# First attention layer of an eight-layer kernel: who masks the early times, and with what

## The chip, the cores and the metric

The kernel runs on one core of one Trainium2 chip. The metric is the time of one execution in microseconds (us) on the device; lower is better. The core's engines each run their own instruction stream: TensorE (PE in the profile), VectorE (DVE), ScalarE (ACT), GpSimd (POOL), and SyncE (SP), which here issues the DMAs. They meet at semaphores: an instruction adds to one when it has finished, and a `wait_ge` holds one engine's stream until the semaphore has reached a value. Everything behind a wait on the same engine waits too.

## The reference

Eight layers follow one another on a residual stream of 2048 times by 128 channels. Only the first, a windowed attention, is touched. Cut to what matters, it computes:

```
delta, nh, bd, hs = 64, 16, 16, 8
disp = (x @ W_disp)  ;  val = (x @ W_val)            # per head
strain = disp[t - delta + 1 + d] - disp[t]           # for d in 0..63
bond_logits = gelu(strain @ W_strain + rel_emb @ W_pos) @ W_bond
damage = sigmoid(gelu(strain @ W_dmg + b_dmg) @ W_dmg_out + b_dmg_out)
logits = bond_logits - 10 * damage
cmask = t - delta + 1 + d >= 0
logits = where(cmask, logits, -inf)
out = softmax(logits, over d) @ windows of val
```

The mask matters only where t is below 63, that is in the first block of 128 times: there, positions d that would lie before time 0 must not count.

## The kernel before, in words

The layer is `bond_attention`. After a set-up (constants, weights, a layer norm and a transpose) one large block does all the work. It is cut into 8 phases, numbered p = 0 to 7: four chunks of 512 times, and for each two halves of the heads (8 heads each, `HH`). A phase has 32 steps (`TPP`), numbered 0 to 31 here, in four groups of 8 (`TPG`). A step makes one tile of differences, 128 partitions by 4 x 512 elements. The whole run of 256 steps is one order that every engine follows.

In each group, steps 0 to 3 are made by GpSimd (L601, one instruction each, into `l0a_diff_pool`) and steps 4 to 7 (`D_AT`) by VectorE (L580, four instructions each, into `l0a_diff_dve`). Each of the two has a ring of four buffers, and may refill one only when TensorE has reduced what was in it. ScalarE takes the tiles strictly in the order of the steps and applies Gelu in place (L633); TensorE reduces each (L455, eight matmuls). After step 5 of the next group VectorE writes a group's logits to `l0a_logits` (L495).

The softmax of a phase is done while the next phase runs. In the loops of TensorE and VectorE a function `tail` says at which step of the phase each part of it is put in. TensorE transposes the logits of the phase before, one block of 128 times after each of steps 5 to 8 (L384). VectorE's `subtract_max` runs at steps 13 to 16, one block b = 0 to 3 each: a maximum over d (L508), then the difference (L510) from PSUM into the SBUF tile `l0a_exps` (E in the code). It is emitted ahead of VectorE's own difference tile of the same step. ScalarE takes the exponential of all four blocks ahead of step 18 (L609), with a table load on either side. SyncE then writes E to a band in DRAM and reads it back, and TensorE transposes what came back (L392) at steps 28 to 31 and 0 to 3, with VectorE's copies (L518) at steps 4 to 11. ScalarE also makes, ahead of step 26, the tile `l0a_a_of_t` (L616) without which GpSimd can't begin step 0 of the phase after.

The mask: the block b = 0 of the two phases of the first chunk (p = 0 and 1, so in the loop while phases 1 and 2 run) holds the early times. There `subtract_max` first copies the transposed logits from PSUM to E (L505), and GpSimd, which has no access to PSUM in this code, masks E in place with an `affine_select` (L592). GpSimd's stream has this at step 5 of phases 1 and 2, that is between its tile of step 3 and its tile of step 8, with a wait on the copy. VectorE makes that copy at its own step 13. After the mask VectorE takes the maximum and the difference from E in SBUF.

Of the kernel before, what the change touches and what calls it, by code (L numbers as in the profile page):

```python
# [5 lines left out]
P = 128  # L6
# [9 lines left out]
ALU = mybir.AluOpType  # L16
ACT = mybir.ActivationFunctionType
AX = mybir.AxisListType.X
NEG = -1.0e30
# [150 lines left out]
def bond_attention(nc, g, I):  # L170


    NH, HS, BD, W = 16, 8, 16, 64
    HH = P // BD
# [5 lines left out]
    TPP = GPP * TPG  # L180
# [5 lines left out]
    with ExitStack() as ctx:  # L186
        r = Room(nc, ctx, "l0a")
# [10 lines left out]
        V = r.sb("val", [P, TB, NH, HS + 1])  # L198
        VS = r.sb("val_shifted", [P, TB, NH, HS + 1])
        zero = r.sb("zero", [P, HH * UB])  # L200
        band = nc.dram_tensor("l0a_band", [2, 4, P, UB * HH], F32, kind="Internal").ap()
        band_zeroed = r.sem("band_zeroed")
        with ExitStack() as ctx2:
# [35 lines left out]
            sel, zr = r2.sem("mask_steps"), r2.sem("zeroed")  # L239
            with nc.Block() as block:  # L240

                @block.vector
                def _(dve):
                    dve.memset(zero[:, :], 0.0).then_inc(zr, 1)
                    dve.memset(wbs[:, :, :, :], 0.0)
                    dve.memset(A[:, :, :, 0:PAD], 0.0)
                    dve.memset(V[:, :, :, HS:HS + 1], 1.0)
                    dve.memset(VS[:, :, :, HS:HS + 1], 1.0)
                    dve.memset(VS[0:W, 0, :, 0:HS], 0.0)

                @block.gpsimd
                def _(pool):
                    pool.memset(bm[:, :], 1.0).then_inc(sel, 1)
                    pool.wait_ge(sel, 1)
                    pool.affine_select(out=bm[:, :], in_=bm[:, :], compare_op=ALU.is_ge, fill=0.0, base=0,
                                       pattern=[[-BD, HH]], channel_multiplier=1).then_inc(sel, 1)
                    pool.wait_ge(sel, 2)
                    pool.affine_select(out=bm[:, :], in_=bm[:, :], compare_op=ALU.is_ge, fill=0.0, base=BD - 1,
                                       pattern=[[BD, HH]], channel_multiplier=-1)

                @block.sync
                def _(sp):
                    sp.wait_ge(zr, 1)
                    for par in range(2):
                        for b in range(4):
                            sp.dma_start(band[par, b], zero[:, :]).then_inc(band_zeroed, 16)
# [45 lines left out]
        E = r.sb("exps", [P, 4, W, HH])  # L312
# [9 lines left out]
        at_ready, atb_ready = r.sem("a_of_t_in_psum"), r.sem("a_of_t_in_sbuf")  # L322
        filled, emptied = r.sem("ring_filled"), r.sem("ring_emptied")
        maxd, expd = r.sem("max_done"), r.sem("exp_done")
        raw, masked = r.sem("first_block_copied"), r.sem("first_block_masked")
        written, loaded = r.sem("band_written"), [r.sem("band_loaded%d" % b) for b in range(4)]
        v_ps, inv, o_done = r.sem("values_in_psum"), r.sem("sums_inverted"), r.sem("o_done")
        ot_ps, ot_sb, y_ps, x_done = r.sem("oT_in_psum"), r.sem("oT_copied"), r.sem("y_in_psum"), r.sem("x_added")
# [4 lines left out]
        def use(*key):  # L333
            return uses.setdefault(key, len(uses))

        def bank(n):
            return g.ps[:, n * CH:(n + 1) * CH]

        def slot(s):
            i = s // TPG * len(D_AT) + D_AT.index(s % TPG) if s % TPG in D_AT else s // TPG * NP_ + s % TPG  # L340
            return (dd[:, i % ND, :, :], diff_dve, i) if s % TPG in D_AT else (dp[:, i % NP_, :, :], diff_pool, i)

        def place(s):
            p, rest = divmod(s, TPP)
            dg, rest = divmod(rest, TPG)
            k, n = divmod(rest, 4)
            return p, p // 2, p % 2, dg, k, n

        def window(s):
            p, q, hf, dg, k, n = place(s)  # L350
            first = A[:, hf, k, q * CH + 16 * dg + n + 1:q * CH + 16 * dg + n + 2]
            return bass.AP(first.tensor, first.offset, [list(first.ap[0]), [4, 4], [1, CH]])

        with nc.Block() as block:

            @block.tensor
            def _(pe):
# [90 lines left out]
                for s in range(NT):  # L448
                    p, q, hf, dg, k, n = place(s)
                    ge, _, _ = slot(s)  # L450
                    pe.wait_ge(gelu_done, s + 1)
                    if n == 0 and s >= TPG:
                        pe.wait_ge(tanh_done if k == 0 else logit_done, s // TPG)
                    for c in range(4):
                        mm = pe.matmul(g.ps[32 * c:32 * c + 32, (2 + k) * CH:(3 + k) * CH], wbs[:, k, n, :], ge[:, c, :],  # L455
                                       start=(n == 0), stop=(n == 3))
                    mm.then_inc(reduced, 1)
                    tail(p, s % TPP)
# [5 lines left out]
            def _(dve):  # L464
# [33 lines left out]
                def subtract_max(p, b):  # L498
                    u = use("l", p, b)
                    dve.wait_ge(filled, u + 1)  # L500
                    if b == 0 and p >= 1:
                        dve.wait_ge(written, 32 * p)
                    raw_l = bank(RING[u % len(RING)]).rearrange("p (d h) -> p d h", h=HH)
                    if p // 2 == 0 and b == 0:
                        dve.tensor_copy(E[:, 0, :, :], raw_l).then_inc(raw, 1)  # L505
                        dve.wait_ge(masked, p + 1)
                        raw_l = E[:, 0, :, :]
                    dve.tensor_reduce(mx[:, b, :], raw_l.rearrange("p d h -> p h d"), AX, ALU.max).then_inc(maxd, 1)  # L508
                    dve.wait_ge(maxd, LB * p + b + 1)
                    dve.tensor_tensor(E[:, b, :, :], raw_l, mx[:, b, :].unsqueeze(1).broadcast_to([P, W, HH]),  # L510
                                      ALU.subtract).then_inc(emptied, 1)
# [53 lines left out]
                for s in range(NT):  # L565
                    p, q, hf, dg, k, n = place(s)
                    if s % TPP == 0:
                        a_of_t(p)
                    tail(p, s % TPP)
                    if s % TPG not in D_AT:  # L570
                        continue
                    out, _, i = slot(s)
                    if s % TPP == D_AT[0]:
                        dve.wait_ge(at_ready, p + 1)
                    if i >= ND:
                        dve.wait_ge(reduced, (i - ND) // ND * TPG + D_AT[i % ND] + 1)
                    src = window(s)
                    for c in range(4):
                        d = 16 * dg + 4 * c + n
                        ins = dve.scalar_tensor_tensor(out[:, c, :], src[:, c, :], pos[:, d:d + 1], bank(1), ALU.add, ALU.subtract)  # L580
                    ins.then_inc(diff_dve, 1)
# [4 lines left out]
            @block.gpsimd  # L586
            def _(pool):
                for s in range(NT):
                    p, q, hf, dg, k, n = place(s)
                    if s % TPP == 5 and 1 <= p <= 2:  # L590
                        pool.wait_ge(raw, p)
                        pool.affine_select(out=E[:, 0, :, :], in_=E[:, 0, :, :], compare_op=ALU.is_ge, fill=NEG,  # L592
                                           base=1 - W, pattern=[[1, W], [0, HH]], channel_multiplier=1).then_inc(masked, 1)
                    if s % TPG in D_AT:
                        continue
                    out, _, i = slot(s)
                    if s % TPP == 0:
                        pool.wait_ge(atb_ready, p + 1)
                    if i >= NP_:
                        pool.wait_ge(reduced, (i - NP_) // NP_ * TPG + i % NP_ + 1)  # L600
                    pool.tensor_tensor(out, window(s), atb[:, p % 2, :].unsqueeze(1).broadcast_to([P, 4, CH]),  # L601
                                       ALU.subtract).then_inc(diff_pool, 1)
# [1821 lines left out]


LAYERS = (bond_attention, masked_ffn, mamba, gated_experts, dual_attention, ternary_ffn, plain_attention, int8_ffn)


# [58 lines left out]
```

## Time and profile before

| | us |
|---|---|
| median of 3 runs | 3114.46 |
| lowest and highest | 3110.84, 3115.29 |
| the profiled execution | 3105.74 |
| its span in the trace | 3103.7 |
| block of the first attention in the trace (8 phases, then the last softmax) | 39.8 to about 645 |
| busy over the whole span: PE, DVE, ACT, POOL | 77%, 62%, 64%, 34% |

The busy shares are means over eight layers with different limits, so they do not say what the first one is worth; for that the block has to be read by itself. In the block POOL is busy for 534 us. An engine that ends an instruction frees the next one's start, and for pipelined instructions the end of one and the start of the next can overlap by some 0.1 us.

### The profile page before, as it was taken

Reading aid. Unit: us, or ns where it says so; the run is one execution under the profiler, and the core shown is the slowest. Engines: PE = TensorE matmul, PEld = TensorE weight load, DVE = VectorE, ACT = ScalarE, POOL = GpSimd, SP = SyncE. Lnnn points to the kernel's source line nnn. Section 1 sums busy time; section 2 is a strip of 40 time slices with the busy share of each in tenths; the row PEclk is TensorE's granted clock in tenths of the full one; section 3 lists DMA queues with packets and bytes.
Section 4 is the critical chain, followed back from the end, with each engine's and each line's share of the span. In section 5 each row is a group of like instructions: output and inputs, shape, how many; then the busy total and the mean of one; then the engine's idle time right before and its main releaser. Section 6 shows DMA issues by size and latency. Waiting matters only on the chain. (4 is left out here: it accounts for less than half of the span.)

```text
span 3103.7 us, 32934 instructions
## 1 busy us (share of the span) xinstructions
PE 2384.6 (77%) x12512; PEld 823.1 (27%) x12512; DVE 1938.8 (62%) x2732; ACT 1977.1 (64%) x1894; POOL 1068.9 (34%) x404
## 2 busy tenths in 40 slices
PE   3577777756546676755799988999769859999995
PEld 1122222333112222322222242222434412222223
DVE  5777988758699999887598907986350430121115
ACT  4789999912523333212499947997522249999991
POOL 5889999711079998621000400013000000000000
PEclk8889999979678888887899999999889879999998
DMA  2011121110044544201301020001010030111000
GB/s 72 1 41 41 44 77 43 41 51 8 7 159 156 172 156 153 71 9 54 63 11 26 11 39 1 11 13 43 7 39 0 20 75 14 31 29 26 14 6 27
DMA packets 67032, 144.68 MB, mean 47 GB/s; under 512 B 15607, under 2 KB 30032, under 8 KB 66161
## 3 DMA queue, kind: packets, MB, share of 16 engines
q1 hardware_dynamic: 66864, 142.46, 16.4%
q8 instruction: 103, 1.69, 0.2%
q14 instruction: 65, 0.52, 0.1%
HBM read 117.99 MB, written 24.25 MB: 46 GB/s over the span
## 5 line engine op out<-in xcount | busy, mean ns | idle before, releaser
L601 POOL TENSOR_TENSOR l0a_diff_pool<-l0a_A,l0a_a_of_t 128x2048 f32<-128x2048 f32 x128 | 532.4, 4197 | 34.8 <-ACT l0a_a_of_t L616 34.8
L1604 ACT ACTIVATE l2x_pT<-ps 128x1024 f32<-128x1024 f32 x512 | 495.8, 1021 | 7.3 <-PE ps L1563 5.4
L1604 ACT ACTIVATE l3he_pT<-ps 128x1024 f32<-128x1024 f32 x512 | 496.0, 1021 | 4.1 <-PE ps L1563 2.2
L1069 PE MATMUL ps<-l1s_hc,all_ident 128*128 128x512 f32 x512 | 283.7, 707 | 182.6 <-POOL l1s_hc L1040 100.3
L580 DVE SCALAR_TENSOR_TENSOR l0a_diff_dve<-l0a_A,l0a_pos,ps 128x512 f32<-128x512 f32 x512 | 344.7, 740 | 44.2 <-PE ps L455 44.1
L1031 POOL TENSOR_TENSOR l1s_dBx<-l1a_dtx,l1s_Bs 128x1024 f32<-128x1024 f32 x128 | 297.4, 2353 | 133.3 <-DMA l1s_Bs<-l1a_bc 133.3
L1055 ACT ACTIVATE ps<-l1a_dt,l1a_A 128x1024 f32<-128x1024 f32 x128 | 143.1, 1118 | 274.0 <-DVE l1s_hc L1100 219.9
L1667 DVE COPY l3he_oT<-ps 128x512 f32<-128x512 f32 x16 | 11.1, 691 | 445.2 <-PE ps L1577 445.1
L1563 PE MATMUL ps<-l3h_Qs,l3h_Ks 75*128 75x512 bf16 x1024 | 267.8, 385 | 24.5 <-DVE ps L1652 24.5
L1563 PE MATMUL ps<-l2m_Qs,l2m_Ks 75*128 75x512 bf16 x1024 | 270.2, 388 | 9.8 <-PEq L1886 9.8
L633 ACT ACTIVATE l0a_diff_pool<-l0a_diff_pool 128x2048 f32<-128x2048 f32 x128 | 237.7, 1901 | 53.9 <-POOL l0a_diff_pool L601 53.8
L1577 PE MATMUL ps<-l2x_pT,l2m_Va 128*9 128x512 f32 x2048 | 269.0, 598 | 1.2 <-ACT l2x_pT L1604 1.2
L1577 PE MATMUL ps<-l3he_pT,l3h_Va 128*9 128x512 f32 x2048 | 268.4, 596 | 0.6 <-ACT l3he_pT L1604 0.6
L455 PE MATMUL ps<-l0a_diff_pool,l0a_reducers 128*32 128x512 f32 x1024 | 158.2, 702 | 119.3 <-ACT l0a_diff_pool L633 118.1
L2028 POOL TENSOR_TENSOR l2s_E<-l2s_E,l2x_rest 128x2048 f32<-128x2048 f32 x16 | 72.7, 4545 | 510.6 <-DVEq L1752 505.5
L633 ACT ACTIVATE l0a_diff_dve<-l0a_diff_dve 128x2048 f32<-128x2048 f32 x128 | 237.2, 1897 | 0.3
L1713 DVE TENSOR_SCALAR_CACHE_REDUCE l2x_rest<-l2s_E,l2x_at 128x2048 f32<-128x2048 f32 x96 | 225.2, 2346 | 3.4
L1069 PEld LDWEIGHTS ps<-l1s_hc,all_ident 128*128 128x128 f32 x512 | 109.1, 224 | 357.9 <-POOL l1s_hc L1040 133.4
L455 PE MATMUL ps<-l0a_diff_dve,l0a_reducers 128*32 128x512 f32 x1024 | 150.0, 664 | 50.3 <-ACT l0a_diff_dve L633 48.8
L1563 PEld LDWEIGHTS ps<-l3h_Qs,l3h_Ks 75*128 75x128 bf16 x1024 | 79.8, 98 | 305.3 <-ACT l3he_pT L1604 218.9
L1563 PEld LDWEIGHTS ps<-l2m_Qs,l2m_Ks 75*128 75x128 bf16 x1024 | 80.4, 98 | 292.6 <-ACT l2x_pT L1604 218.3
L1100 DVE TENSOR_TENSOR l1s_hc<-ps,l1s_Cs 128x1024 f32<-128x1024 f32 x86 | 105.3, 1224 | 1.8 <-issue 0.3
(404 smaller groups left out, 3321.8 us busy)
## 6 DMA issues: line engine op xcount, KB each, us to landing
l1s_Bs<-l1a_bc SPq DMA_DIRECT2D x64, 512.0 KB, 3.7
l1s_Cs<-l1a_bc SPq DMA_DIRECT2D x64, 512.0 KB, 4.7
l0a_band_rows<-l0a_band SPq DMA_DIRECT2D x32, 512.0 KB, 5.3
l0a_band<-l0a_exps SPq DMA_DIRECT2D x16, 512.0 KB, 5.1
l2m_Ks<-l2m_parts SPq DMA_DIRECT2D x36, 128.0 KB
l2m_Qs<-l2m_parts SPq DMA_DIRECT2D x72, 64.0 KB
l3h_Ks<-l3h_parts SPq DMA_DIRECT2D x36, 128.0 KB
l3h_Qs<-l3h_parts SPq DMA_DIRECT2D x72, 64.0 KB
```

Of the source, the lines that this page charges most:

```text
L455: mm = pe.matmul(g.ps[32 * c:32 * c + 32, (2 + k) * CH:(3 + k) * CH], wbs[:, k, n, :], ge[:, c, :], start=(n == 0), stop=(n == 3))
L580: ins = dve.scalar_tensor_tensor(out[:, c, :], src[:, c, :], pos[:, d:d + 1], bank(1), ALU.add, ALU.subtract)
L601: pool.tensor_tensor(out, window(s), atb[:, p % 2, :].unsqueeze(1).broadcast_to([P, 4, CH]), ALU.subtract).then_inc(diff_pool, 1)
L633: act.activation(ge, ge, ACT.Gelu).then_inc(gelu_done, 1)
L1031: pool.tensor_tensor(db[:, m % NDB, :], dtx[:, i, h, half * TH:(half + 1) * TH], Bs[:, k % NBS, :], ALU.mult).then_inc(dbd, 1)
L1055: act.activation(hpair(m), dt[:, i, h, half * TH:(half + 1) * TH], ACT.Exp, scale=Al[:, i, h, n:n + 1]).then_inc(dad, 1)
L1069: mm = pe.matmul(g.ps[:, (4 + 2 * h + q) * CH:(5 + 2 * h + q) * CH], g.ident[:, :], hc[:, m % NHC, q * CH:(q + 1) * CH], start=(n == 0), s ...
L1100: dve.tensor_tensor(hc[:, m % NHC, :], hpair(m), Cs[:, k % NCS, :], ALU.mult).then_inc(weighed, 1)
L1563: mm = pe.matmul(g.ps[:, slot * QC + c * CH:slot * QC + (c + 1) * CH], hd.Ks[:, hg % 2, j, kt * P:(kt + 1) * P], hd.Qs[:, qc, j, c * CH:(c ...
L1577: mm = pe.matmul(g.ps[32 * j:32 * j + HS + 1, ACC + c * CH:ACC + (c + 1) * CH], hd.Va[:, kt, hg * 4 + j, :], pT[:, (4 * n + j) % NPT, c * ...
L1604: act.activation(pT[:, turn % NPT, :], g.ps[:, slot * QC:(slot + 1) * QC], ACT.Exp).then_inc(expd, 1)
L1713: step(dve.tensor_scalar(junk[:, b % 2, :], E[:, b, :], at[:, 0, b:b + 1], 0.0, ALU.is_ge, ALU.add, accum_out=at[:, 1, b:b + 1]))
```

## The change

The tile `early_mask` (128 x 64: 0 where the position counts, -1e30 where it does not) is made once in the layer's set-up block by GpSimd, with a memset and an `affine_select`. In the loop VectorE no longer copies the logits to E; it adds the mask tile, repeated over the heads, to them on the way from PSUM to E. GpSimd's `affine_select` and its wait on the copy are gone from its stream, and the semaphore for that copy with them. The maximum and the difference from E stay.

```
+        early = r.sb("early_mask", [P, W])
...
+                    pool.memset(early[:, :], 0.0).then_inc(sel, 1)
+                    pool.wait_ge(sel, 3)
+                    pool.affine_select(out=early[:, :], in_=early[:, :], compare_op=ALU.is_ge, fill=NEG, base=1 - W,
+                                       pattern=[[1, W]], channel_multiplier=1)
...
                     if p // 2 == 0 and b == 0:
-                        dve.tensor_copy(E[:, 0, :, :], raw_l).then_inc(raw, 1)
+                        dve.tensor_tensor(E[:, 0, :, :], raw_l, early[:, :].unsqueeze(2).broadcast_to([P, W, HH]),
+                                          ALU.add).then_inc(masked, 1)
                         dve.wait_ge(masked, p + 1)
                         raw_l = E[:, 0, :, :]
...
-                    if s % TPP == 5 and 1 <= p <= 2:
-                        pool.wait_ge(raw, p)
-                        pool.affine_select(out=E[:, 0, :, :], in_=E[:, 0, :, :], compare_op=ALU.is_ge, fill=NEG,
-                                           base=1 - W, pattern=[[1, W], [0, HH]], channel_multiplier=1).then_inc(masked, 1)
```

## Rows read from the trace of the kernel before

**Rows 1.** Waits in 30 to 645 us: who waited for whom, total, times, longest.

```profile
POOL l0a_exps L592 <- DVE l0a_exps L505: 25.9, 2, 13.5
```

**Rows 2.** Timeline of POOL: start, us, instruction, count, [idle before it, and who ended it].

```profile
39.80 82.90 POOL L601 TENSOR_TENSOR l0a_diff_pool<-l0a_A,l0a_a_of_t 128x2048 f32<-128x2048 f32 x20 [31.47 <-ACT l0a_a_of_t L616]
135.12 1.09 POOL L592 TENSOR_SCALAR_AFFINE_SELECT l0a_exps<-l0a_exps 128x512 f32<-128x512 f32 x1 [12.42 <-DVE l0a_exps L505]
136.17 50.16 POOL L601 TENSOR_TENSOR l0a_diff_pool<-l0a_A,l0a_a_of_t 128x2048 f32<-128x2048 f32 x12
186.78 16.67 POOL L601 TENSOR_TENSOR l0a_diff_pool<-l0a_A,l0a_a_of_t 128x2048 f32<-128x2048 f32 x4 [0.45 <-ACT l0a_a_of_t L616]
...
217.96 50.16 POOL L601 TENSOR_TENSOR l0a_diff_pool<-l0a_A,l0a_a_of_t 128x2048 f32<-128x2048 f32 x12
268.57 66.52 POOL L601 TENSOR_TENSOR l0a_diff_pool<-l0a_A,l0a_a_of_t 128x2048 f32<-128x2048 f32 x16 [0.46 <-ACT l0a_a_of_t L616]
335.67 66.49 POOL L601 TENSOR_TENSOR l0a_diff_pool<-l0a_A,l0a_a_of_t 128x2048 f32<-128x2048 f32 x16 [0.58 <-ACT l0a_a_of_t L616]
```

**Rows 3.** Windows over phases 1, 2, 3: length, busy by engine, PE clock, DMA share, GB/s.

```profile
106.90:186.80 79.90, 49.13 (x272) 8.99 (x272) 54.37 (x78) 63.30 (x40) 67.03 (x18) 0.75 0.13 40
186.80:268.60 81.80, 54.63 (x452) 18.16 (x448) 61.94 (x91) 65.68 (x41) 67.89 (x18) 0.83 0.12 39
268.60:335.70 67.10, 50.33 (x456) 18.29 (x452) 59.87 (x94) 65.45 (x41) 66.52 (x17) 1.00 0.15 48
```

**Rows 4.** Timeline of ACT in phase 4, steps 11 on, to the next phase.

```profile
436.11 1.91 ACT L633 ACTIVATE l0a_diff_pool<-l0a_diff_pool 128x2048 f32<-128x2048 f32 x1 [1.53 <-POOL l0a_diff_pool L601]
437.93 3.69 ACT L633 ACTIVATE l0a_diff_dve<-l0a_diff_dve 128x2048 f32<-128x2048 f32 x2
...
442.10 3.87 ACT L633 ACTIVATE l0a_diff_dve<-l0a_diff_dve 128x2048 f32<-128x2048 f32 x2
445.87 3.70 ACT L633 ACTIVATE l0a_diff_pool<-l0a_diff_pool 128x2048 f32<-128x2048 f32 x2
...
469.10 0.71 ACT L616 ACTIVATE l0a_a_of_t<-l0a_A,l0a_minus_bd 128x512 f32<-128x512 f32 x1
```

**Rows 5.** Timeline of DVE in phase 4, steps 13 to 15.

```profile
431.47 0.69 DVE L495 SCALAR_TENSOR_TENSOR l0a_logits<-l0a_tanh,ps 128x512 f32<-128x512 f32 x1 [0.72 <-PE ps L455]
432.07 0.68 DVE L508 TENSOR_REDUCE l0a_maxima<-ps 128x8 f32<-128x512 f32 x1
...
433.40 2.72 DVE L580 SCALAR_TENSOR_TENSOR l0a_diff_dve<-l0a_A,l0a_pos,ps 128x512 f32<-128x512 f32 x4
...
441.31 2.71 DVE L580 SCALAR_TENSOR_TENSOR l0a_diff_dve<-l0a_A,l0a_pos,ps 128x512 f32<-128x512 f32 x4
```

**Rows 6.** Timeline of DVE in phase 1, around the first mask.

```profile
133.68 0.69 DVE L495 SCALAR_TENSOR_TENSOR l0a_logits<-l0a_tanh,ps 128x512 f32<-128x512 f32 x1 [2.46 <-PE ps L455]
134.28 0.68 DVE L505 COPY l0a_exps<-ps 128x512 f32<-128x512 f32 x1
136.24 1.09 DVE L508 TENSOR_REDUCE l0a_maxima<-l0a_exps 128x8 f32<-128x512 f32 x1 [1.27 <-POOL l0a_exps L592]
137.36 3.86 DVE L510 TENSOR_TENSOR l0a_exps<-l0a_exps,l0a_maxima 128x512 f32<-128x512 f32 x1
```

**Rows 7.** Line 510 by form: count, duration ns min/median/max, first and last start.

```profile
L510 DVE TENSOR_TENSOR l0a_exps<-ps,l0a_maxima x30: 690/691/692, 144.5 to 627.3; 128x512 f32<-128x512 f32 x30
L510 DVE TENSOR_TENSOR l0a_exps<-l0a_exps,l0a_maxima x2: 3861/3862/3862, 137.4 to 219.2; 128x512 f32<-128x512 f32 x2
```

**Rows 8.** Timeline of ACT in phase 1: the first Gelu after the mask.

```profile
140.71 1.91 ACT L633 ACTIVATE l0a_diff_pool<-l0a_diff_pool 128x2048 f32<-128x2048 f32 x1 [8.29 <-POOL l0a_diff_pool L601]
```

**Rows 9.** Timeline of PE: one step's eight matmuls, behind its Gelu.

```profile
267.94 1.06 PE L455 MATMUL ps<-l0a_diff_pool,l0a_reducers 128*32 128x512 f32 x8 [0.74 <-ACT l0a_diff_pool L633]
```

**Rows 10.** Timeline of the set-up block: the last mask step of before, and SyncE's DMA issues.

```profile
8.14 0.19 POOL L258 TENSOR_SCALAR_AFFINE_SELECT l0w_bm<-l0w_bm 128x8 f32<-128x8 f32 x1
...
8.93 7.65 SPq L266 DMA_DIRECT2D l0a_band<-l0a_zero  x8
```

More of the change, by code:

```diff
@@ L324, in bond_attention @@
         maxd, expd = r.sem("max_done"), r.sem("exp_done")
-        raw, masked = r.sem("first_block_copied"), r.sem("first_block_masked")
+        masked = r.sem("first_block_masked")
         written, loaded = r.sem("band_written"), [r.sem("band_loaded%d" % b) for b in range(4)]
```

## The prediction

> **What bounds the kernel now.** I read the table of waits over the first attention first. One entry belongs to the changed lines: GpSimd's mask L592 waits for VectorE's copy L505, 25.9 us in two waits [rows 1]. An idle engine costs only if it is the one that paces, so next comes GpSimd's own timeline [rows 2]. It shows an engine with nothing else missing: 20 tiles in one piece from 39.80 to 122.70, then a hole, the mask, 12 tiles, then four tiles to 203.45, a second hole, the mask, 12 tiles, and from phase 3 on 16 tiles in one piece per phase, 66.5 us, with half a microsecond between phases. Phase 3 is 335.67 - 268.57 = 67.10 us long. Phase 1 starts at 122.70 less four tiles (16.6) = 106.1 and lasts to 186.78, so 80.7; phase 2 lasts 81.8. The windows say the same: the same POOL work, 67.0, 67.9 and 66.5 us, in 79.9, 81.8 and 67.1 [rows 3]. So GpSimd stands still in phases 1 and 2, and nothing covers it.
>
> But GpSimd is not alone. The half microsecond at each phase's start is ended by ScalarE's L616 [rows 2], and ScalarE is busy for 65.45 of 67.10 us [rows 3]. The timeline of ScalarE in phase 4, which has the same parity as phase 2, shows how the two share the pace [rows 4]: ScalarE waits 1.53 us for GpSimd's tile of step 11 at 436.11, which is 33.3 us after the phase's start, and from there it runs without a hole to L616 at 469.10, 0.78 before GpSimd can start phase 5. So between step 11 and step 26 ScalarE has no slack: whatever makes it late there moves the next phase by as much.
>
> **The change part by part.** *What goes.* The wait and the mask on GpSimd: from 122.70 to 136.17 is 13.5 us, from 203.45 to 217.96 is 14.5 us [rows 2], 28.0 together (my sum of phase lengths, 80.7 + 81.8 less twice 67.1, says 28.3, the same within reading). This would be the gain if all else went as in phase 3.
>
> *What does not go.* At the masked block VectorE still takes its maximum and difference from SBUF. The maximum takes 1.09 us against 0.68 from PSUM [rows 6, 5]. The difference takes 3.86 us both times, where the 30 that read PSUM take 0.69 [rows 7]. The 3.86 is not work. It was issued at 137.36 and ended at 141.22 [rows 6], while GpSimd's tile begun at 136.17 [rows 2] was just done: ScalarE took it at 140.71 [rows 8]. The difference ended 0.5 us behind that tile, about its own length. So I read it as held until the running GpSimd tile is over. Before, this lay in GpSimd's own hole and cost little; now it stands in the stretch where ScalarE has no slack.
>
> The Trainium skill, page "SBUF — State Buffer", section "SBUF: two separate sides", has a rule for this: VectorE and GpSimd share one pair of SBUF ports as an exclusive lock, which a VectorE instruction with two SBUF inputs needs too, and whoever starts first keeps it for the whole instruction. The trace agrees: 3.86 against 0.69 us. By that rule the difference is held again and the gain is the smaller one below; were there no such lock it would be the full 28.
>
> *Phase 1, worked out.* Until 122.70 nothing changes. GpSimd then makes its tiles of steps 8 to 11 without a hole, the last over by 106.1 + 33.3 = 139.4, so begun at about 139.4 - 4.2 = 135.2. VectorE writes the logits at 133.68 as before, since those depend on ScalarE's steps up to 7. The add starts where the copy did, 134.28. I take 0.69 for it, from the difference that also reads PSUM and an SBUF tile with a repeated dimension [rows 7]; bounds are the copy's 0.68 and the 3.86 of the held one. The maximum starts at 134.95 and ends at 136.05; the wait on `masked` is now one of VectorE for itself, met when the add ends. The difference is issued at 136.1, inside the tile of step 11, and ends at 139.4 + 0.5 = 139.9. Queued behind wait and difference on VectorE are its tiles of steps 13, 14, 15, each with one `subtract_max` in front; steps 13 to 15 start 7.91 us apart [rows 5] and a tile takes 2.71. So they start at 139.85, 143.8 and 147.75, and that of step 15 is ready at 150.45. ScalarE, paced as in phase 4, starts step 11 at 139.4, step 14 at 145.4, step 16 at 139.4 + 9.76 = 149.2 [rows 4]. It needs step 15 at about 147.3; it gets it at 150.5 and reaches step 16 one Gelu (1.8) later, at 152.3: 3.1 late. From there to L616 it is 469.10 - 445.87 = 23.23 us, so 175.5, and GpSimd starts phase 2 at 176.3, where it was 186.78. **Gain 10.5.**
>
> *Phase 2.* In the times of phase 4: logits at 431.47, add at 432.07, maximum at 432.75, difference issued at 433.9, inside the tile of step 11 that is over at 436.05; it ends at 436.6. Tile 13 then starts at 436.55 in place of 433.40, tile 15 at 444.5, ready at 447.2. ScalarE reaches step 16 at 449.05, not 445.87: 3.2 late. The phase is 67.1 + 3.2 = 70.3 in place of 81.8. **Gain 11.5.** Phase 3 starts at 246.6 in place of 268.57.
>
> *The rest at nothing.* GpSimd's ring does not stop it before: for step 24 (155.9 in phase 1) it needs step 16 reduced, at about 155.3 (152.3, a Gelu of 1.9, matmuls of 1.1 [rows 8, 9]), and it ends the phase waiting for L616 anyway. The band's DMAs hang on the exponential, and so do the transposes behind; both move with ScalarE. The two new set-up instructions go behind L258, which ends at 8.33; at 0.2 us each they are done near 8.9, and the block lasts until SyncE has issued its eight DMAs at 16.58 [rows 10]. Without that cover they would cost 0.5. All buffers made after the mask tile move by 256 bytes; no row prices that, and I take nothing.
>
> *Sum.* 10.5 + 11.5 = **22.0 us** less. Against the profiled execution, 3105.74 - 22.0 = 3083.7. That execution is 8.7 below the median of the runs; against the median the forecast is 3114.46 - 22.0 = **3092.5**. Bounds: if the difference is held by nobody and VectorE has slack, nothing is late, gain 28, 3086.4. If the add is held as well, or GpSimd's next tile gets in ahead, each lateness grows by a tile of 4.15, gain 22.0 - 8.3 = 13.7, 3100.8. I take 22.0 since the row that it rests on is the same instruction in the same place, 3.86 both times.
>
> **The rivals.** *The full gain.* VectorE's lateness is absorbed or the difference slips between two tiles: 28.0 less, 3086.4. For it: in phase 1 the issue at 136.1 is only 0.9 behind the change of tiles. Against: in phase 4 even an undelayed tile of step 15 makes ScalarE's pair take 3.87 in place of 3.69 [rows 4], so there is no reserve.
>
> *The clock (slower than before).* TensorE's granted clock was 0.75 and 0.83 in phases 1 and 2 and 1.00 in phase 3 [rows 3]. If the new rhythm left it at the lower level (1.2 GHz) for a phase, phase 3's 50.3 us of matmuls would take up to 100.7, and TensorE would set a phase at 33.6 above 67.1. One such phase in full gives 3114.46 - 22.0 + 33.6 = 3126; it decides from two thirds of a phase on. Against: the low means fall together with the lulls that go away, and the phases without a lull have the high clock.
>
> *Given back.* The gain is there in the block but a stall of the same kind comes behind it, for example GpSimd held at its ring by TensorE late at the masked phases, or a later layer falls on the other clock level: about no change, 3114. Nothing in the rows of phases 3 and 4 shows such a stall, and the layers behind begin from a common barrier.
>
> **How the numbers follow.** My forecast 70 in 100 (its own range 3087 to 3098), full gain 20, given back 6, the clock 4. A difference below 0.2%, 6.2 us, can't be told from none here; so faster 0.90, same 0.06, slower 0.04. The range takes in both bounds, 3086.4 and 3100.8, with some us for the level of the runs, which among themselves spread over 4.5: 3083 to 3102.
>
> **What would show it.** After the change GpSimd should have 20 + 12 tiles in one piece from 39.80 to about 172.6, then a wait of 3 to 4 us for L616; phase 2 should start at 176 and phase 3 at 247. The difference L510 from SBUF should still take 3 to 4 us twice, and ScalarE should wait for VectorE's tiles at steps 14 and 15 by about 3 us in each of the two phases. A phase 2 that starts at 173 says that the lateness is hidden; L510 at 0.69 that nothing holds it; a start past 180 that the add or the ring costs more. The forecast is wrong in kind if phases 3 to 7 are no longer 67.1, or if the time behind the block changes.

## The result and the profile after

The kernel became slower, by 0.4%. Median of 20 runs 3127.99 us (3119.68 to 3145.51), against 3118.95 us (3108.06 to 3127.09) in 20 runs of the kernel before; ratio 1.0036, 95% interval 1.0022 to 1.0049. The forecast was 3092.5, which is 22.0 under the 3114.46 of the three runs known then. The profiled execution took 3119.74 us, its span 3117.6.

The timeline of POOL after the change, which answers to [rows 2]:

```profile
39.86 115.96 POOL L603 TENSOR_TENSOR l0a_diff_pool<-l0a_A,l0a_a_of_t 128x2048 f32<-128x2048 f32 x28 [31.01 <-ACT l0a_a_of_t L618]
176.96 83.53 POOL L603 TENSOR_TENSOR l0a_diff_pool<-l0a_A,l0a_a_of_t 128x2048 f32<-128x2048 f32 x20 [21.14 <-PE ps L460]
263.80 49.91 POOL L603 TENSOR_TENSOR l0a_diff_pool<-l0a_A,l0a_a_of_t 128x2048 f32<-128x2048 f32 x12 [3.31 <-ACT l0a_a_of_t L618]
```

The hole at 122.70 is gone, as wanted: 28 tiles in one piece. But then GpSimd stands for 21.14 us, and not for ScalarE's L618 (the L616 of before) but for TensorE, that is for a free buffer. The second masked phase, the rest of these rows, is as forecast: no hole, and 3.31 us of waiting for L618 at its end, where 3 to 4 were forecast. From GpSimd's first tile to phase 3 it is 263.80 - 39.86 = 223.9 us, before 268.57 - 39.80 = 228.8: 4.8 us gained where 22.0 were forecast.

VectorE's timeline around the first mask, which answers to [rows 6]; L510 is the new add, L516 the difference:

```profile
134.72 0.69 DVE L500 SCALAR_TENSOR_TENSOR l0a_logits<-l0a_tanh,ps 128x512 f32<-128x512 f32 x1 [3.42 <-PE ps L460]
135.32 0.68 DVE L510 TENSOR_TENSOR l0a_exps<-ps,l0a_early_mask 128x512 f32<-128x512 f32 x1
136.04 1.12 DVE L514 TENSOR_REDUCE l0a_maxima<-l0a_exps 128x8 f32<-128x512 f32 x1
137.19 19.18 DVE L516 TENSOR_TENSOR l0a_exps<-l0a_exps,l0a_maxima 128x512 f32<-128x512 f32 x1
156.29 2.71 DVE L586 SCALAR_TENSOR_TENSOR l0a_diff_dve<-l0a_A,l0a_pos,ps 128x512 f32<-128x512 f32 x4
```

One instruction of 19.18 us, which read in the same way took 3.86 before [rows 7]. It ended at 156.37; GpSimd's 28 tiles ended at 155.82. So it was passed over at four boundaries between GpSimd's tiles and ran when GpSimd had stopped. By form, the instructions that touch E:

```profile
L516 DVE TENSOR_TENSOR l0a_exps<-ps,l0a_maxima x30: 690/691/693, 159.6 to 623.0; 128x512 f32<-128x512 f32 x30
...
L510 DVE TENSOR_TENSOR l0a_exps<-ps,l0a_early_mask x2: 683/683/683, 135.3 to 222.2; 128x512 f32<-128x512 f32 x2
...
L516 DVE TENSOR_TENSOR l0a_exps<-l0a_exps,l0a_maxima x2: 3342/11259/19176, 137.2 to 224.1; 128x512 f32<-128x512 f32 x2
```

The add costs 0.68, where 0.69 was forecast, and the second difference 3.34, inside the forecast's 3 to 4. ScalarE, which answers to [rows 4]:

```profile
141.18 1.89 ACT L635 ACTIVATE l0a_diff_dve<-l0a_diff_dve 128x2048 f32<-128x2048 f32 x1
159.04 1.91 ACT L635 ACTIVATE l0a_diff_dve<-l0a_diff_dve 128x2048 f32<-128x2048 f32 x1 [15.96 <-DVE l0a_diff_dve L586]
...
162.99 1.91 ACT L635 ACTIVATE l0a_diff_dve<-l0a_diff_dve 128x2048 f32<-128x2048 f32 x1 [1.47 <-DVE l0a_diff_dve L586]
166.95 1.91 ACT L635 ACTIVATE l0a_diff_dve<-l0a_diff_dve 128x2048 f32<-128x2048 f32 x1 [2.05 <-DVE l0a_diff_dve L586]
168.77 3.69 ACT L635 ACTIVATE l0a_diff_pool<-l0a_diff_pool 128x2048 f32<-128x2048 f32 x2
...
191.98 0.71 ACT L618 ACTIVATE l0a_a_of_t<-l0a_A,l0a_minus_bd 128x512 f32<-128x512 f32 x1
```

The reader sees the loop close. VectorE's tile of step 13 is behind the held difference, ScalarE takes tiles in order and stands 15.96 us for it, TensorE gets nothing to reduce, so no buffer of GpSimd's comes free; GpSimd goes on until its four are full, and only that lets VectorE in. No run has another number of buffers, so what a longer ring would do is not shown.

The profile before and the first one after differ by 13.9 us in span although the block is shorter. The stretch from the second layer norm's L125 to the end of the span took 2442.3 us before and 2460.5 after. It took 2456.0 in `e2_tile_only` below, whose loop is the old one, and 2448.3 to 2464.6 in the eleven other profiles. So a range of some 20 us lies in the layers behind whatever the first one does, and one profile's span against another's says nothing here of a change of 10 us. The block must be compared by itself, and the kernels by their medians.

### The profile page after: what moved, and what is told of

The parts are those of the page before. It is cut to its first block and busy times, and to the rows that moved or that the text cites. A ratio compares the mean times of both kernels' runs of the same rounds, so it can differ in the third digit from the quotient of the medians.

```text
span 3117.6 us, 32933 instructions
## 1 busy us (share of the span) xinstructions
PE 2394.7 (77%) x12512; PEld 825.3 (26%) x12512; DVE 1953.8 (63%) x2732; ACT 1976.8 (63%) x1894; POOL 1066.7 (34%) x404
```

## The experiments

Two theories stood at the start. **Held:** the difference that reads two SBUF tiles is passed over while GpSimd's tiles follow each other without a hole; the number of tiles varies, and most runs have two long holds. **Rest:** the block is always some 5 us shorter and the loss lies in the layers behind. "Block" below is the time from GpSimd's first tile to the start of phase 3.

| kernel | masked difference (L510 before, L516 after), us | block | median of runs | of before beside it | ratio, 95% interval |
|---|---|---|---|---|---|
| before | 3.86, 3.86 | 228.8 | | | |
| after | 19.18, 3.34 | 223.9 | 3127.99 | 3118.95 | 1.0036 (1.0022 to 1.0049) |
| e1_again | 20.15, 19.83 | 240.8 | 3128.61 | 3116.48 | 1.0029 (1.0009 to 1.0049) |
| e2_tile_only | 3.87, 3.87 | 228.8 | 3119.12 | 3116.48 | 1.0005 (0.9985 to 1.0024) |
| e3_in_psum | none | 201.0 | 3090.19 | 3116.48 | 0.9916 (0.9889 to 0.9942) |
| e4_hole_at_16 | 3.68, 2.72 | 206.8 | 3092.69 | 3116.48 | 0.992 (0.9893 to 0.9947) |
| e5_max_in_psum | 0.69, 0.69 | 201.7 | 3091.52 | 3118.18 | 0.9914 (0.9891 to 0.9937) |

**The changed kernel again, no edit.**

> The changed kernel once more, for a second profile and its time beside the variants. Theory 'held': the difference L516 that reads two SBUF tiles is passed over by GpSimd's tiles for as long as they follow without a hole, by chance at each boundary; so its two durations come out anew, between 3 and 20 us, and the start of phase 3 lies between 246 (both short) and 281 (both long). The time of the runs says most of them have at least one long hold: ratio to before 1.000 to 1.006. Rival 'rest': the block is always about 4 us shorter, as in the first profile, and the loss of 9 us in the median comes from the layers behind; then L516 is again 19 and 3 us, phase 3 starts at 264, and the stretch from the second layer norm (657) to the end is again some 14 us or more longer than before's 2442.

The differences from SBUF by form, as above (count, then duration in ns, min, median, max):

```profile
L516 DVE TENSOR_TENSOR l0a_exps<-l0a_exps,l0a_maxima x2: 19827/19986/20145, 137.3 to 225.5; 128x512 f32<-128x512 f32 x2
```

POOL's timeline in this execution:

```profile
178.33 66.42 POOL L603 TENSOR_TENSOR l0a_diff_pool<-l0a_A,l0a_a_of_t 128x2048 f32<-128x2048 f32 x16 [21.47 <-PE ps L460]
261.28 8.32 POOL L603 TENSOR_TENSOR l0a_diff_pool<-l0a_A,l0a_a_of_t 128x2048 f32<-128x2048 f32 x2 [16.54 <-PE ps L460]
```

This time both are long, GpSimd stands twice for buffers, and the block is 12.0 us longer than before, about what the medians say (12.1 here, 9.0 in the first comparison). The first profile had shown the milder case. The twelve runs reach from 3103.83 to 3139.62; whether the lowest one had two short holds, no profile shows. "Rest" has fallen as far as the block goes.

**The old loop with the mask tile and its two set-up instructions.** Edit: only `early = r.sb(...)` and the memset and `affine_select` of the change.

> The kernel before plus only the mask tile in memory and the two set-up instructions that make it; the loop is the old one. Theory 'held': nothing changes, ratio 1.000 within 0.0015, difference from SBUF 3.86 us twice, phase 3 starts at 268.6. Rival 'rest' (the shift of all later buffers by 256 bytes, or the set-up, slows something): 1.002 to 1.005.

No difference that can be measured, and the block is the same to 0.1 us. Neither the set-up nor the shift of the buffers behind plays a part.

**The mask added in place in PSUM.**

```
                     if p // 2 == 0 and b == 0:
-                        dve.tensor_tensor(E[:, 0, :, :], raw_l, early[:, :].unsqueeze(2).broadcast_to([P, W, HH]),
+                        dve.tensor_tensor(raw_l, raw_l, early[:, :].unsqueeze(2).broadcast_to([P, W, HH]),
                                           ALU.add).then_inc(masked, 1)
                         dve.wait_ge(masked, p + 1)
-                        raw_l = E[:, 0, :, :]
```

> The mask tile is added in place in PSUM, and maximum and difference then read PSUM as in the other blocks; nothing reads two SBUF tiles. Theory 'held': no instruction of VectorE takes over 1 us there, GpSimd has no hole in phases 1 and 2, phase 3 starts at 240.5 (28 us earlier than before), the ratio is 0.991 (0.989 to 0.993). Rival 'rest': the block gains 28 but the layers behind lose 9 to 14, ratio 0.994 to 0.996. Rival 'another limit' (ScalarE or the ring): phase 3 starts later than 245.

VectorE at the mask, then POOL's timeline:

```profile
134.10 0.69 DVE L510 TENSOR_TENSOR ps<-ps,l0a_early_mask 128x512 f32<-128x512 f32 x1
134.82 0.69 DVE L513 TENSOR_REDUCE l0a_maxima<-ps 128x8 f32<-128x512 f32 x1
135.55 0.69 DVE L515 TENSOR_TENSOR l0a_exps<-ps,l0a_maxima 128x512 f32<-128x512 f32 x1
```

```profile
39.60 132.64 POOL L602 TENSOR_TENSOR l0a_diff_pool<-l0a_A,l0a_a_of_t 128x2048 f32<-128x2048 f32 x32 [30.80 <-ACT l0a_a_of_t L617]
172.75 66.50 POOL L602 TENSOR_TENSOR l0a_diff_pool<-l0a_A,l0a_a_of_t 128x2048 f32<-128x2048 f32 x16 [0.52 <-ACT l0a_a_of_t L617]
240.56 66.52 POOL L602 TENSOR_TENSOR l0a_diff_pool<-l0a_A,l0a_a_of_t 128x2048 f32<-128x2048 f32 x16 [1.31 <-ACT l0a_a_of_t L617]
```

The full gain: 27.8 us in the block, 26.3 in the medians, and this version beats both kernels. The layers behind take nothing back.

**A hole for VectorE.** GpSimd waits at step 16 for the difference:

```
+                    if s % TPP == 16 and 1 <= p <= 2:
+                        pool.wait_ge(emptied, use("l", p - 1, 0) + 1)
```

> The changed kernel, with one wait more: GpSimd waits ahead of its tile of step 16 in phases 1 and 2 for the difference of the masked block, so that a hole comes at most one tile after it is issued. Theory 'held': L516 takes 3 to 4 us both times and GpSimd then stands for about 0.7 us; ScalarE late by some 3 us as first forecast, phase 3 starts at 247, ratio 0.993 (0.991 to 0.995). Rival 'rest': as far as the block goes the same, but the ratio stays above 0.997. Rival 'something else holds L516' (the mask tile, the self wait): it stays at 19 us in phase 1.

POOL's timeline in phases 1 and 2 and on to phase 3:

```profile
138.62 16.64 POOL L605 TENSOR_TENSOR l0a_diff_pool<-l0a_A,l0a_a_of_t 128x2048 f32<-128x2048 f32 x4 [0.63 <-DVE l0a_exps L516]
158.40 49.89 POOL L605 TENSOR_TENSOR l0a_diff_pool<-l0a_A,l0a_a_of_t 128x2048 f32<-128x2048 f32 x12 [3.14 <-PE ps L460]
208.92 33.22 POOL L605 TENSOR_TENSOR l0a_diff_pool<-l0a_A,l0a_a_of_t 128x2048 f32<-128x2048 f32 x8 [0.63 <-DVE l0a_exps L516]
245.25 66.49 POOL L605 TENSOR_TENSOR l0a_diff_pool<-l0a_A,l0a_a_of_t 128x2048 f32<-128x2048 f32 x16 [3.11 <-ACT l0a_a_of_t L620]
```

A wait *added* to the changed kernel, of 0.63 us twice, gains 36 us in the medians. The block is 22.0 us shorter than before, to a tenth the sum of my forecast: this is the kernel that I had forecast, one in which the hold ends with the running tile.

**One SBUF input in place of two.** The masked block's maxima go to PSUM, E stays:

```
+                    m = mx[:, b, :]
+                    if p // 2 == 0 and b == 0:
+                        m = bank(RING[u % len(RING)])[:, 0:HH]
...
```

The maximum (L514 of the changed kernel) then writes `m`, and the difference reads it.

> The changed kernel, but the masked block's maxima are written to PSUM (the first 8 columns of the block's own bank, which the add has freed), so that the difference reads one SBUF tile (E, written just before, as in the changed kernel) and PSUM. Theory 'two SBUF inputs': it is held no longer, L516's form takes 0.7 to 1.1 us, phase 3 starts at 241 to 242 (VectorE late by 1.1 us at most), ratio 0.9915 (0.989 to 0.994). Rival 'any SBUF tile that is shared in time with GpSimd' or 'E itself': still held for 3 to 20 us, phase 3 at 247 or later, ratio 0.993 to 1.004.

The masked differences by form:

```profile
L519 DVE TENSOR_TENSOR l0a_exps<-l0a_exps,ps x2: 686/686/687, 136.9 to 205.2; 128x512 f32<-128x512 f32 x2
```

The same E, just written, and 0.69 us, though both were issued inside a running GpSimd tile: the first in the 24th tile since the last hole, where the changed kernel's were held for 19 to 20 us in every profile. So it is the second SBUF tile, here of eight numbers per partition, and not E, that exposes the instruction.

**Four pieces.** The difference in four instructions of 128 columns.

> The changed kernel with the masked block's difference cut in four instructions of 128 columns. Theory 'held whole': the first piece bears the wait (3 to 20 us), and after a long one, when GpSimd has run out of buffers, the other three take 0.15 to 0.3 us each; after a short one the next pieces may be held again. Rival 'the two share the port and both slow down': all four pieces take about a quarter of the whole each, and GpSimd's tiles beside them are longer than 4.15 us.

The four pieces of the first masked phase by form (in the second, the first piece took 19.11):

```profile
L519 DVE TENSOR_TENSOR l0a_exps<-l0a_exps,l0a_maxima x4: 277/278/19770, 136.4 to 156.5; 128x128 f32<-128x128 f32 x4
```

In the first masked phase the first piece takes 19.77 and the rest 0.28 each. It waits whole and then runs at full speed. GpSimd's 28 tiles up to there took 115.99 us, as in the profile after (115.96), so they were not slowed either: the two do not share.

**Eight masked blocks.** The detour over E in all phases, from the second chunk on with zeros.

> The changed kernel with the add and the detour over E for block 0 in all eight phases (from the second chunk on with a tile of zeros, which changes nothing): eight differences that read two SBUF tiles, seven beside GpSimd's unbroken tiles, the last one after GpSimd has ended. Theory 'held by chance at each boundary': the last takes 0.7 to 1.1 us, which is the unheld length; of the seven each takes about 0.5 us more than the rest of one, or two, ... or of all GpSimd tiles until GpSimd runs out of buffers, at most 20 us; most are over 15. Each long one costs its phase 17 to 21 us against 67.1, so the kernel is 60 to 130 us slower than the one before, ratio 1.02 to 1.04. Rival 'phase 1 alone is special' (its first long hold comes from something that only the start has): holds of 3 to 4 us from phase 3 on, ratio 0.998 to 1.003.

VectorE's timeline, the first four of the eight differences:

```profile
137.20 20.16 DVE L519 TENSOR_TENSOR l0a_exps<-l0a_exps,l0a_maxima 128x512 f32<-128x512 f32 x1
225.29 19.85 DVE L519 TENSOR_TENSOR l0a_exps<-l0a_exps,l0a_maxima 128x512 f32<-128x512 f32 x1
312.70 2.68 DVE L519 TENSOR_TENSOR l0a_exps<-l0a_exps,l0a_maxima 128x512 f32<-128x512 f32 x1
383.42 19.84 DVE L519 TENSOR_TENSOR l0a_exps<-l0a_exps,l0a_maxima 128x512 f32<-128x512 f32 x1
```

The three that follow are 19.20, 19.82 and 19.23, and the eighth, with GpSimd at its end, 0.69: that is the length without a hold. Ratio 1.0239 (1.0198 to 1.028). No hold in any profile was between 6 and 19 us: it ended at the first boundary, or not before GpSimd stopped.

**What decides between the two?** Before the change the difference got in at the first boundary four times out of four (two profiles), and there GpSimd had stood just ahead. So I gave it a hole again, at several distances, in the kernel with eight masked blocks. Directly ahead of the tile in which the difference is issued:

```
+                    if s % TPP == 11 and p >= 1:
+                        pool.wait_ge(masked, p)
```

> As e6_eight, but GpSimd waits ahead of its tile of step 11 in every phase for the masked add, so that it stands for about a microsecond and starts that tile just before the difference is issued, as it did in the kernel before (a hole, one tile, then the boundary at which the difference got in, four times out of four). It tells what decides at a boundary. Theory A 'a hole just before lets VectorE in at the first boundary': all seven differences take 3 to 5 us, the kernel costs about 1 to 5 us per phase, ratio 0.998 to 1.005. Theory B 'chance alone': several are over 8 us, ratio over 1.01.

All eight by form; the 691 ns is the one after GpSimd's end:

```profile
L519 DVE TENSOR_TENSOR l0a_exps<-l0a_exps,l0a_maxima x8: 691/4001/4008, 136.3 to 626.6; 128x512 f32<-128x512 f32 x8
```

Seven of seven are 3.98 to 4.01; ratio 1.0027 (1.0010 to 1.0044) in place of 1.0239. The next three move the hole away by a tile each (`reduced`, `TPP * p + 7`, `+ 5`, `+ 3`, ahead of steps 10, 9, 8):

> As e7_eight_hole, but GpSimd's hole is ahead of its tile of step 10 (it waits there for TensorE's reduction of step 6, which ends about 0.5 to 0.8 us after GpSimd could start). So the difference is issued within the second tile after a hole, not the first. Theory 'the hole must be right before' (order is lost with the first tile that follows another without a hole): most of seven differences take 19 to 20 us. Theory 'a hole restores order for some tiles' (something drifts apart slowly): most take the rest of the tile, 3 to 5 us.

> The hole (0.3 to 0.5 us) is ahead of step 9, so the difference is issued within the third tile after it. Theory 'right before': 19 to 20 us in most of seven. Theory 'slow drift': a mixture, more long ones than with the hole at step 10.

> The hole (about 1 us, none in phase 1) is ahead of step 8, so the difference is issued within the fourth tile after it. Theory 'right before': as without a hole, 19 to 20 us in most of seven. Theory 'slow drift': nearly as without one, still more short ones than the 2 of 13 seen so far.

With the hole at 10 all seven took 4.17 to 4.57, at 9 4.18 to 5.02. At 8 six took 3.63 to 4.39, and the one of phase 1, where the wait was already met and no hole came, 20.14. VectorE's timeline there, the first two:

```profile
134.81 20.14 DVE L519 TENSOR_TENSOR l0a_exps<-l0a_exps,l0a_maxima 128x512 f32<-128x512 f32 x1
222.52 4.38 DVE L519 TENSOR_TENSOR l0a_exps<-l0a_exps,l0a_maxima 128x512 f32<-128x512 f32 x1
```

"The hole must be right before" is out. Farther away:

> As e11_hole_at_8, but the hole lies farther ahead, at another distance by phase: ahead of step 3 in phases 1, 4 and 7 (the difference is then issued within the fifth tile after it), of step 2 in phases 2 and 5 (sixth tile), of step 1 in phases 3 and 6 (seventh). GpSimd waits there for a reduction of the phase before that ends 0.3 to 2.3 us after it could start. Theory 'slow drift' (with each tile that follows another without a hole, VectorE's chance at a boundary falls): some are long; most likely the short ones are among the fifths, the long ones among the sevenths. Rival 'a fixed reach of four': all seven are 19 to 20 us.

VectorE's timeline, the differences of phases 3, 4, 6 and 7:

```profile
303.45 3.31 DVE L519 TENSOR_TENSOR l0a_exps<-l0a_exps,l0a_maxima 128x512 f32<-128x512 f32 x1
374.93 19.84 DVE L519 TENSOR_TENSOR l0a_exps<-l0a_exps,l0a_maxima 128x512 f32<-128x512 f32 x1
...
542.33 3.33 DVE L519 TENSOR_TENSOR l0a_exps<-l0a_exps,l0a_maxima 128x512 f32<-128x512 f32 x1
613.22 3.12 DVE L519 TENSOR_TENSOR l0a_exps<-l0a_exps,l0a_maxima 128x512 f32<-128x512 f32 x1
```

This went only partly as set up: in phases 1 and 4 no hole came, in 2 and 5 a second one came just ahead of the difference. What is left, the seventh tile twice (303.45, 542.33) and the fifth once (613.22), was short; I had expected the sevenths long. All differences with two SBUF inputs beside running tiles, by how many tiles had followed without a hole, the running one counted (a hole is 0.28 us or more; e4 is left out, since its hole comes behind):

| tile in which it is issued, since the last hole | let in at the first boundary |
|---|---|
| 1st to 4th | 33 of 33 |
| 5th to 7th | 3 of 3 |
| 8th | 1 of 3 |
| 12th | 1 of 7 |
| 24th | 0 of 6 |

So what counts is how long GpSimd has run unbroken. "A fixed reach of four" is out, and one chance for all tiles too. A chance that falls with each unbroken tile fits, but what changes in that time was not shown, nor is its course between the 8th tile and the 12th clear from so few cases.

## Why the prediction was wrong

**The failed step** is the one on L510 of before: "So I read it as held until the running GpSimd tile is over." The hold was seen rightly, as was its cause, and that it now stood where ScalarE has no slack. Its length was taken from two rows that agreed to the nanosecond, 3.86 us, and both had been measured in the first tile behind the very hole that the change removes. The prediction says that the difference of before "lay in GpSimd's own hole"; its own rows say otherwise: GpSimd was making tiles again from 136.17, and the difference began at 137.36 [rows 2, 6]. "The same instruction in the same place" was false in what mattered: its neighbour had been made to stand just before. In the changed loop it was 19 to 20 us in five cases of six, five tiles and not one. Put into the forecast's own working for phase 1, it gives the profile: the difference ends at 156.4, ScalarE reaches step 16 at 168.77, and L618 follows 23.21 later, at 191.98.

**The bound** failed with it. I had allowed for GpSimd's next tile "ahead" once, 4.15 us per phase, and no row gave a reason for once. The bound that the code gives is the ring: GpSimd can run on until its buffers are full, up to step 19, which is where it stopped in every long hold. Two such holds make the block of e1 34.0 us longer than the 206.8 of the forecast. That is the slower side, which I had given to the clock alone, at 4 in 100.

The Trainium skill, page "SBUF — State Buffer", section "SBUF: two separate sides", says that whoever starts first has the shared ports for its whole instruction. The runs agree as far as that goes (0.69 with one SBUF input, 2.7 to 20 with two). I had read into it that the waiting one has them next; the profile after shows it passed over four times.

**What was right:** the hole of 28 us and that nothing covered it (e3 gained 27.8 in the block); ScalarE as the second pacer, with the lateness moving L618 one for one; the add at 0.69, the set-up and the 256 bytes at nothing (e2); phase 2 after a short hold, 70.2 us long (GpSimd's tiles of 193.56 and 263.80 begin it and phase 3) where 70.3 was forecast; and phases 3 to 6, 268.8 us together where they were 268.4. The clock rival did not occur: TensorE's granted clock was 0.75 in phase 1 of the profile after and 0.90 in phase 2, against 0.75 and 0.83 before [rows 3], and in phase 1 TensorE was busy for 48.8 of 87.4 us, so it did not set the pace; and in e1, with both long holds, the block alone accounts for 12.0 of the 12.1 us.

**Open:** what in GpSimd's unbroken run shuts VectorE out, and how often a timed run of the changed kernel has two, one or no long hold; three profiles of its loop (after, e1, e8) show five long and one short.

## What to carry to other kernels

Where VectorE reads two SBUF tiles beside a GpSimd that works without a pause, don't count the rest of one instruction but, as the bound, all that GpSimd can still do before it must wait; here the ring set that. Give the instruction one input in PSUM (0.69 us here for up to 20) or give GpSimd a wait on it. And when a change removes a stall, no duration measured beside that stall may be taken over: the stall may have been what kept it short.

## What was not expected of the hardware

- A VectorE instruction of 0.69 us was held for 19.2 to 20.2 us (a piece of 0.28 us for 19.1 and 19.8) by five GpSimd instructions in a row, though there were four boundaries between them; over all kernels but e4, 14 of 16 differences issued in the 8th tile or later were held until GpSimd had run out of buffers; the other two got in at the next boundary.
- In 36 of 36 cases within the first seven tiles behind a hole of 0.28 us or more, it got in at the next boundary.
- A second input of eight numbers per partition (the maxima) is enough to expose an instruction; moving those eight to PSUM ends it (0.69 us, twice).
- The instruction that gets in holds GpSimd up in turn: in the profile after, the GpSimd tile behind the short hold took 5.07 us, and the same tile of e1, where the difference was passed over, 4.57.
